# A graph network on one core: the slices' total weights summed by ScalarE as it copies the turned weights, in place of products with ones

## The reference

```python
slice_weights = softmax((x_mid @ W_slice + b_slice) / temp, axis=-1)          # 8 heads, 6250 nodes, 64 slices
slice_norm    = slice_weights.sum(axis=2)                                     # sum over the nodes
slice_token   = einsum('bhnc,bhng->bhgc', fx_mid, slice_weights)
slice_token   = slice_token / (slice_norm[..., None] + 1e-05)
...                                                                           # attention among the 64 tokens of a head
out_x         = einsum('bhgc,bhng->bhnc', out_slice, slice_weights)           # back to the nodes
```

## Time and profile before

| | us |
|---|---|
| three executions | 4424.64, 4429.74, 4432.52 |
| median | 4429.74 |
| span of the profiled execution | 3913.9 |

### The profile page before, as it was taken

The page is one execution under the profiler, slowest core; times in us unless marked ns, Lnnn a source line. Parts: engine busy times, 40 slices in busy tenths (PEclk is TensorE's granted clock), DMA queues, the critical chain, the costliest instruction groups (busy, mean ns, idle before and its releaser), DMA issues. The chain is left out here.

```text
span 3913.9 us, 41587 instructions
## 1 busy us (share of the span) xinstructions
PE 2817.2 (72%) x12730; PEld 2139.6 (55%) x12730; DVE 1759.8 (45%) x4424; ACT 768.9 (20%) x1634; POOL 2555.5 (65%) x2689
## 2 busy tenths in 40 slices
PE   3577877777768647667777777665677777777778
PEld 2466656656544535556555555544466555556557
DVE  6433335555524842443333333332355555555533
ACT  1111101111103313321111111110122222222210
POOL 3677777777760342557777777775777777777701
PEclk9999988888879879889989999887889999999969
DMA  4344434444433457754444444433344444444405
GB/s 139 116 117 120 124 107 139 130 138 131 129 96 94 143 164 202 213 179 133 138 117 125 124 125 125 114 111 97 109 123 122 124 124 123 123 121 125 125 21 197
DMA packets 279533, 501.68 MB, mean 128 GB/s; under 512 B 59771, under 2 KB 179969, under 8 KB 279162
## 3 DMA queue, kind: packets, MB, share of 16 engines
q0 software_dynamic: 126240, 345.85, 30.9%
q1 hardware_dynamic: 135916, 139.10, 11.5%
q10 hardware_dynamic: 17136, 13.84, 1.1%
HBM read 419.12 MB, written 79.18 MB: 127 GB/s over the span
## 5 line engine op out<-in xcount | busy, mean ns | idle before, releaser
L1476 PE MATMUL bank<-g,m 128*128 128x256 f32 (+1 forms) x4704 | 1466.0, 436 | 806.4 <-DMA g<-d_t,src_i 537.4
L1399 POOL DMA_INDIRECT g<-d_t,src_i x1568 | 1505.2, 960 | 511.4 <-issue 511.4
L1476 PEld LDWEIGHTS bank<-g,m 128*128 128x128 f32 x4704 | 879.6, 211 | 1102.3 <-issue 400.1
L1399 POOL DMA_INDIRECT g<-d_xn,src_i x784 | 802.3, 1023 | 244.3 <-issue 242.5
L1424 DVE TENSOR_SCALAR m<-iota,rel_f,ew_f 128x128 f32<-128x128 f32 x1568 | 421.6, 365 | 255.9 <-PE bank L1476 250.4
L1440 DVE TENSOR_TENSOR accT<-bank,accT 128x256 f32 x294 | 122.8, 418 | 593.1 <-PE bank L1464 592.9
L1405 ACT ACTIVATE s<-bank 128x256 f32<-128x256 f32 (+1 forms) x294 | 111.4, 379 | 1076.0 <-PE bank L1478 554.7
L1427 DVE TENSOR_TENSOR eq<-iota,rel_f 128x1024 bf16<-128x1024 f32 x98 | 119.9, 1224 | 138.3 <-PE bank L1478 138.3
L1478 PE MATMUL bank<-ones_b,eq 128*128 128x1 bf16 x784 | 136.9, 175 | 0.0
L1340 PE MATMUL bank<-wg,side_lg 128*128 128x256 f32 (+1 forms) x392 | 132.1, 428 | 2.9 <-DVE side_lg L1332 2.9
L219 POOL TENSOR_TENSOR rsd<-ved,mhalf 128x2 f32<-128x2 f32 (+1 forms) x25 | 19.0, 760 | 175.6 <-DVE ved L213 175.4
(11 more groups left out here) (387 smaller groups left out, 4273.3 us busy)
## 6 DMA issues: line engine op xcount, KB each, us to landing
g<-d_t,src_i POOLq DMA_INDIRECT x1568, 2.8
side_xn<-d_xn SPq DMA_DIRECT2D x96, 256.0 KB, 3.1
g<-d_xn,src_i POOLq DMA_INDIRECT x784, 2.8
d_swT<-wkv SPq DMA_DIRECT2D x48, 256.0 KB, 3.0
swT<-d_swT SPq DMA_DIRECT2D x24, 512.0 KB, 3.8
xt<-d_xs POOLq DMA_DIRECT2D x80, 128.0 KB, 3.0
d_ys<-y ACTq DMA_DIRECT2D x80, 128.0 KB, 2.6
x<-in_x SPq DMA_DIRECT2D x24, 256.0 KB, 2.7
```

The costliest lines, as they stand in the source:

```text
L1399: pool.indirect_dma_start(g[n % RING][:, u, 0:D], None, table, bass.IndirectOffsetOnAxis(ap=k.src_i[:, t:t + 1], axis=0)).then_inc(gathere ...
L1476: ins = pe.matmul(b[:, 0:GW], m[o][:, u, :], g[r][:, u, :], start=(u == 0), stop=(u == GT - 1 and not count))
```

## The change

The four products with ones of each tile go. The one copy of the turned weights becomes four, one for each block of 128 slices, each of which also writes the sum of its columns (the nodes of the tile) to a column of a new tile `norms` of 128 x 4 x 49, allocated ahead of the second layer's stages. The heads stage adds the 49 columns on VectorE, waits for that, and then takes the totals from there and not from bank 5.

```diff
 def sums(self, i, w):
...
         for q in range(HEADS * SLICES // P):
             sw = lg[0:w, q * P:(q + 1) * P]
-            pe.matmul(k.bank[3 + q // 2][:, q % 2 * D:(q % 2 + 1) * D], sw, self.xn3[i % self.LG][0:w, :], start=(i == 0 and q % 2 == 0), stop=last and q % 2 == 1)
-            ins = pe.matmul(k.bank[5][:, q:q + 1], sw, k.ones[0:w, 0:1], start=(i == 0 and q == 0), stop=last and q == HEADS * SLICES // P - 1)
+            ins = pe.matmul(k.bank[3 + q // 2][:, q % 2 * D:(q % 2 + 1) * D], sw, self.xn3[i % self.LG][0:w, :], start=(i == 0 and q % 2 == 0), stop=last and q % 2 == 1)
         ins.then_inc(self.summed, 1)
...
 def copy_swT(self, i, w):
...
-        act.activation(self.swT[i % 2][:, :, 0:w], self.k.bank[6][:].rearrange("p (q n) -> p q n", n=P)[:, :, 0:w], ACT.Copy).then_inc(self.swT_done, 1)
+        for q in range(HEADS * SLICES // P):
+            ins = act.activation(self.swT[i % 2][:, q, 0:w], self.k.bank[6][:, q * P:q * P + w], ACT.Copy, accum_out=self.k.norms[:, q, i:i + 1])
+        ins.then_inc(self.swT_done, 1)
...
 stage_heads
+        total = st.sb("total", [P, NC4])
...
-                dve.tensor_copy(Tt[:, :, D], k.bank[5][:, 0:NC4]).then_inc(divided, 1)
-                dve.tensor_scalar(rn[:], k.bank[5][:, 0:NC4], 1e-5, None, ALU.add).then_inc(divided, 1)
+                dve.tensor_reduce(total[:], k.norms[:], AX.X, ALU.add).then_inc(added, 1)
+                dve.wait_ge(added, 1)
+                dve.tensor_copy(Tt[:, :, D], total[:]).then_inc(divided, 1)
+                dve.tensor_scalar(rn[:], total[:], 1e-5, None, ALU.add).then_inc(divided, 1)
...
 build
+        k.norms = sb("norms", [P, HEADS * SLICES // P, NTILE])
```

More of the change, by code:

```diff
@@ L2413, in stage_heads @@
         norm = st.sb("norm", [1, HS])
+        total = st.sb("total", [P, NC4])
         rn = st.sb("rn", [P, NC4])
-        divided = st.sem("divided")
+        added, divided = st.sem("added"), st.sem("divided")
         t_read, t_turned, t_out = st.sem("t_read"), st.sem("t_turned"), st.sem("t_out")
```

## The result

| | median us | runs |
|---|---|---|
| before | 4424.64 | 7, 4406.79 to 4432.52 |
| after | 4395.84 | 7, 4381.60 to 4408.48 |

The ratio is 0.9935, with a 95% interval of 0.9913 to 0.9956: 28.8 us less. The forecast was 4430.7, its range 4421.7 to 4439.0, and rival 3 (43 us less, "PE was the bound after all") had a chance of 0.03. So the change is faster and the prediction was wrong.

A forecast was written before the change was run, and what follows sets the result against it. GpSimd's gathers were taken to bound the third aggregation, so only its end and the heads stage counted: -4.19 (ones) + 4.75 (copies) + 0.4 (reduction) = +1.0 us on 4429.74, giving 4430.7, range 4421.7 to 4439.0.

The forecast's parts named there:

- rival 3: Third aggregation: PE was the bound after all, 49 x 0.88 = 43 us less, 4387; chance 0.03.
- as long as gathers go out: Third aggregation up to its last gather: GpSimd's gathers set the time at 1.272 us each, neither PE nor ScalarE.
- 0.95 more: ScalarE's copy of turned weights: four copies with sums take 0.95 us more per tile, five times on the end path.
- the upper bound: ScalarE's four copies: each sum written by a 0.294 us operation, nothing overlapping, 2.20 us, 1.61 more than now.
- The estimate of 0.30 more: ScalarE's four copies, priced by the skill's instruction costs with overlap: 893 ns, 0.30 us more than now.
- Before the end ... covered: Rounds before the last gather: ScalarE's extra time is hidden; without that cover, up to 1.6 us in 44 rounds, 70 us.
- 0.4: Heads stage: the added VectorE reduction of 128x196 and the step to the next operation cost 0.4 us.
- the +0.56: Five rounds after the last gather: copies add 4.75 us, removed products with ones save 4.19.
- Rivals 1: ScalarE's copies overlap and their sums come nearly free: -3.0 us, 4426.7; chance 0.20.
- rival 2: End rounds: each sum is written after its copy drains, making ScalarE's copy the longer link: +4.3 us, 4434.0; chance 0.18.
- Rival 4: PE does too little to keep its clock, falls to 1.2 GHz every round and becomes the bound: 4755; chance 0.02.
- Rival 5: Time around the span follows the number of instructions: about 430 go, 5.3 us less, 4425; chance 0.07.

The follow-up runs named there:

- e2: Changed kernel with the single ScalarE copy restored and a constant in place of the totals, products with ones still gone: 4396.98 against 4427.07, 0.9927.
- e13: Kernel before with only the four products with ones per tile moved from PE's slot 2 to slot 5: 4391.53 against 4418.19, 0.9934.
- e5: Changed kernel with each product of sums widened to 512 columns into bank 5, pooled sums left out: 4423.00 against 4429.36, 0.9990.
- e7: Kernel before with all sums and products with ones moved from PE's slot 2 to slot 5: 4371.23 against 4429.36, 0.9871.
- e8: Changed kernel with the sums moved from PE's slot 2 to slot 5: 4372.24 against 4429.36, 0.9874.
- e6: Changed kernel with 16 one-column memsets per round added in VectorE's wait: 4451.11 against 4429.36, 1.0047.
- e9: Changed kernel with 16 one-column copies per round added in ScalarE's wait: 0.9984 of the kernel before.
- e11: Changed kernel with the sums moved to slot 5 and 16 one-column memsets per round on VectorE: 0.9949 of the kernel before.
- e1: Kernel before, unchanged, timed and profiled again: 4421.51 against 4427.07, 0.9995; its profiled execution took 4413.82 with a span of 4412.3.
- e3: Changed kernel with the products with ones still made but not used: 4438.82 against 4427.07, 1.0026.
- e15: Changed kernel, unchanged, timed again on another chip: 4395.17 against 4418.19, 0.9950.
- e10: Changed kernel with 32 one-column memsets per round added in VectorE's wait: 1.0119 of the kernel before.

## Why the prediction was wrong

**The step that failed** is the first: "as long as gathers go out, time is 1.272 us times their number, and neither PE nor ScalarE sets it". It held in the execution read, where GpSimd waited for nobody, and in no trace of a timed one. The sign was in the prediction's own sum: "the median of the three runs, 4429.74, lies 515.8 us above its span, and I carry that difference unchanged". That difference was not around the span (1.6 us lie there) but a slower pace inside it, with another bound. Rival 3 was weighed down by "GpSimd's gaps, which never exceed 0.3 us"; in timed executions they reach 6.3.

**What stands in its place.** The products with ones were 0.88 us per tile ahead of the turned window on PE, and what waits for that window paces the round. Shown is that their place there costs the time: taking them away (e2), moving them behind (e13) and the change itself all give 0.993 to 0.995; lengthening PE at that place takes most of the gain back (e5); with the sums behind, the change does nothing (e7, e8). A tile gives back some 0.6 us of its 0.88, 29 us over 49 tiles, so rival 3 named the kind of bound and its 43 us were too many. In the window above PE has 44 us less work and waits 18 us more ahead of `turn3` (for VectorE and for nothing named, both rows together), so in these two profiles part of what it saves it waits. Not shown is what in these products costs it, their time or their number: e5 gives the time about a third of the gain, and e6 and e9 to e11 give a price to instructions that take hardly any time.

**The terms, where they can be read.** A product with ones at 0.22 us was right: sum and ones go every 0.66 us in e1, and after, eight records of sums take 1.89 us with no gap. "0.95 more" for the copy was too much. Two of the four copies, and what follows them, on ScalarE after the change:

```profile
3533.14 0.28 ACT L1356 ACTIVATE wkv<-bank 128x128 f32<-128x128 f32 x1 [1.91 <-PE bank L1348]
3533.32 0.20 ACT L1356 ACTIVATION_READ_ACCUMULATOR wkv<-bank 128x1 f32 x1
3533.41 0.27 ACT L1356 ACTIVATE wkv<-bank 128x128 f32<-128x128 f32 x1
...
3534.07 0.22 ACT L1356 ACTIVATION_READ_ACCUMULATOR wkv<-bank 128x1 f32 x1
3534.30 1.28 ACT L1322 ACT_TABLE_LOAD   x1
```

From the first copy to the next operation it is 3534.30 - 3533.14 = 1.16 us, against 3555.37 - 3554.75 = 0.62 for the single copy in e1, so 0.54 more. Each sum is written by an operation of its own, as the upper bound had it, but these overlap the copies. By the Trainium skill, "VectorE: DVE Perf Modes", section "Two Vector instructions with no wait between them", an operation on VectorE that also writes out its accumulator is two instructions; these rows show the same on ScalarE, at 0.20 us a read. The estimate of 0.30 more that the prediction worked out from the Trainium skill, "ScalarE: Activation LUTs", section "What ACT_TABLE_LOAD costs", was nearer to 0.54 than the 0.95 of its sum. "Before the end ... covered" held for the time of the copies: e2 lies only 0.0008 to 0.0023, 4 to 10 us, under the two measurements of the changed kernel, within their intervals. In e3 ScalarE's part cost 11.7 us, 34 ns for each of its 343 more instructions.

**The end.** After, the last gather begins at 4201.03 and the heads stage at 4270.07:

```profile
4201.03 0.95 POOL L1400 DMA_INDIRECT g<-d_t,src_i  x1 [0.30 <-issue]
...
4270.07 0.36 DVE L2422 TENSOR_REDUCE total<-norms 128x4 f32<-128x196 f32 x1 [8.77 <-PEq L95]
4270.46 0.17 DVE L2424 COPY Tt<-total 128x4 f32<-128x4 f32 x1
```

The reduction and its step take 4270.46 - 4270.07 = 0.39; "0.4" was right. The end itself took 69 us here and 80.6 in e1, against 57.4 in the execution read the earlier trace rows, and 65 to 87 in the other profiles of timed executions, so the +0.56 that was forecast for it (4.75 - 4.19) can't be seen. Nor can the gain be shared out by stages from two profiles: two of the changed kernel have 1194.0 and 1175.4 us for the third aggregation.

**The other rivals.** Rivals 1 and 2 put the bound where the forecast put it, and fall with it; the copy's 1.16 us is over rival 1's 0.75 and under rival 2's 2.2. Rival 4 did not come by the change: the clock in the window is 0.82 before (e1), and 0.80 and 0.82 in the two profiles of the changed kernel (after, e15). But the fall that it tells of was there before the change: in the timed executions the clock falls to 1.2 GHz about once a round, as shown above, and they come nowhere near that rival's 4755. Rival 5, fewer instructions, has something in it, as e6 and e10 show, but inside the span and not around it. The change takes 784 records of PE and PEld away and adds 344, so 440 go (41587 and 41147 in the heads of the pages); at 24 to 60 ns that would be 11 to 26 of the 29 us. Against it stand e13, which has the gain with no record gone, and e8, which has the 440 gone and is no faster than e7.

**What stays open** is why PE's updates come 10 us late in most rounds, why VectorE's memsets are held 0.7 us apart in e10, and why the execution read before had no late updates. Its trace holds 60,428 semaphore updates and e1's, of the same program, 26,327 (of these 53,838 and 21,012 are landings of DMA; the instructions are 41587 in both); so the recording itself is a suspect. By the Trainium skill, "NOTIFIC — the notification-queue block", section "7.1 Overflow: three behaviours, one of which stalls the engine", when a ring of records is full, the new record is dropped, the oldest is overwritten, or the engine that makes records is held until software has emptied the ring. Fewer updates in the slower executions would agree with lost records, and instructions held at a fixed step with a held engine; no run here shows that either is the cause, and none was made without recording.

## What to carry to other kernels

Compare the span of a profile with the times of the runs before trusting its bound: where they differ by more than a few us, take another profile, since here a bound that was read at another pace said nothing about the time. Then look for what stands on an engine's queue ahead of the one instruction that others wait for, and move it behind: that cost nothing here and gave as much as the change (e13), and with all of the sums twice as much (e7, 0.9871).

## What the hardware showed beside that

A 1x1 product between 128x128 ones costs PE 0.31 us (0.74 less the 0.435 of a plain product), more than the 0.22 of a 128x1 one, and its weight load's row has 0.33 us of idle before it. Sixteen one-column instructions a round in VectorE's idle time cost 47 us over a stage of 49 rounds, where one instruction of the same total length cost none. And of 32 such instructions that wait for nothing named, those behind the first 13 to 26 start about 0.70 us apart, or twice that (e10: 285 and 112 of 408 steps).
